# Cross-attention and ternary FFN on one core: the first context block loaded in rows and turned by TensorE, its projection in contraction halves

## What is computed

```python
q = ctx @ Wq.T + bq                    # 512 x 128, key likewise with Wk, bk
attention = softmax(q @ key.T)         # 512 x 512
x = x + layernorm(x) @ attention.T
w1q, w2q = ternary(w1), ternary(w2)    # clip(round(w / mean|w|), -1, 1)
h = gelu(layernorm(x) @ w1q.T + b1)    # 512 x 2048
x = x + h @ w2q.T + b2
```

## Time and profile before

| | us |
|---|---|
| median of 3 runs | 312.29 |
| lowest, highest | 311.95, 313.38 |
| profiled execution | 312.49 |
| its span (first to last instruction) | 310.70 |
| TensorE busy | 303.9 |
| VectorE, ScalarE, GpSimd busy | 153.7, 143.9, 109.2 |

### The profile page before, as it was taken

The page is one execution under the profiler, slowest core; times in us unless marked ns, Lnnn a source line. Parts: engine busy times, 40 slices in busy tenths (PEclk is TensorE's granted clock), DMA queues, the critical chain, the costliest instruction groups (busy, mean ns, idle before and its releaser), DMA issues.

```text
span 310.7 us, 3674 instructions
## 1 busy us (share of the span) xinstructions
PE 303.9 (98%) x1401; PEld 144.2 (46%) x1401; DVE 153.7 (49%) x295; ACT 143.9 (46%) x253; POOL 109.2 (35%) x111
## 2 busy tenths in 40 slices
PE   6799999999999999999999999999999999999996
PEld 3366544444444444444444444444444444444455
DVE  0888896764598853755308342445433003442101
ACT  2179998577723506542654604545440017762000
POOL 0276339999979960000903620000650000000000
PEclk9999999999999999999999999999999999999999
DMA  7899999674653992000032854000034100000011
GB/s 174 237 381 408 361 277 205 131 135 103 121 104 63 155 228 105 2 0 0 0 70 54 166 103 154 0 0 0 2 69 115 56 34 0 0 2 0 34 49 54
DMA packets 66706, 32.24 MB, mean 104 GB/s; under 512 B 59504, under 2 KB 60032, under 8 KB 66176
## 3 DMA queue, kind: packets, MB, share of 16 engines
q1 hardware_dynamic: 66368, 31.73, 40.4%
q10 hardware_dynamic: 320, 0.27, 0.4%
HBM read 15.21 MB, written 4.19 MB: 62 GB/s over the span
## 4 chain that ended last, share of the span: by engine, by line
PE 96%; DMA 2%; DVE 1%; SPq 0%; ACT 0%; issue 0%
PE ps_t L511 36%; PE ps_e L536 24%; PE ps_e L494 13%; PE ps_e L525 9%; PE ps_e L443 5%; PE ps_e L435 2%; PE ps_e L543 2%; PE ps_t L435 2%; DMA ctx_sb<-in_ctx 2%; PE ps_t L467 1%; PE ps_e L454 1%; PE ps_t L454 1%; SPq L247 0%; DVE ctxT L764 0%; ACT qkT L644 0%; DVE x_sb L1055 0%
## 5 line engine op out<-in xcount | busy, mean ns | idle before, releaser
L511 PE MATMUL ps_t<-x2T,w1T 128*128 128x512 f16 x512 | 112.1, 379 | 0.0
L706 ACT ACTIVATE ps_t<-ps_t,b_col 128x512 f32<-128x512 f32 x64 | 42.5, 665 | 96.6 <-PE ps_t L511 96.6
L511 PEld LDWEIGHTS ps_t<-x2T,w1T 128*128 128x128 f16 x512 | 50.1, 98 | 60.7 <-issue 0.6
L900 DVE SCALAR_TENSOR_TENSOR gT_lo<-ps_t,h_scale,gT_hi 128x512 f16<-128x512 f32 x64 | 45.1, 746 | 66.2 <-ACT gT_hi L711 66.2
L536 PE MATMUL ps_e<-w_raw,gT_hi 128*128 128x512 f16 x176 | 66.7, 379 | 0.0
L536 PE MATMUL ps_e<-w_raw,gT_lo 128*128 128x512 f16 x176 | 66.7, 379 | 0.0
L349 POOL TENSOR_TENSOR rstd<-var_eps,minus_half 128x4 f32<-128x4 f32 (+1 forms) x9 | 8.5, 947 | 99.7 <-DVE neg_mean L813 99.7
L711 ACT ACTIVATE gT_hi<-ps_t,h_scale 128x512 f16<-128x512 f32 x64 | 40.3, 684 | 0.0
L906 DVE SCALAR_TENSOR_TENSOR x_sb<-ps_e,h_unscale,x_sb 128x512 f32<-128x512 f32 x15 | 11.0, 748 | 57.9 <-PE ps_e L536 54.6
L536 PEld LDWEIGHTS ps_e<-w_raw,gT_lo 128*128 128x128 f16 x176 | 17.2, 98 | 21.4 <-issue 1.0
L536 PEld LDWEIGHTS ps_e<-w_raw,gT_hi 128*128 128x128 f16 x176 | 17.2, 98 | 21.1 <-issue 0.7
(11 more groups left out here) (86 smaller groups left out, 290.9 us busy)
## 6 DMA issues: line engine op xcount, KB each, us to landing
w_raw<-in_L_ffn_w SPq DMA_DIRECT2D x8, 1024.0 KB, 14.7
x_sb<-in_x SPq DMA_DIRECT2D x4, 1024.0 KB, 7.5
out<-x_sb SPq DMA_DIRECT2D x15, 256.0 KB, 2.6
ctx_sb<-in_ctx SPq DMA_DIRECT2D x16, 128.0 KB, 3.2
b_sb<-in_L_ffn_b SPq DMA_DIRECT2D x1, 256.0 KB, 7.2
w_raw<-w_raw SPq DMA_TRANSPOSE x16, 3.8
out<-x_sb SPq DMA_DIRECT2D x2, 128.0 KB, 1.7
x2n<-in_L_xattn_Wq ACTq DMA_DIRECT2D x1, 128.0 KB, 3.0
```

Source lines behind the costliest of these rows:

```text
L511: mm = nc.tensor.matmul(ps_t[t][:], w1T[:, k, j], x2T[:, b % 2, v, :, j], start=(v == 0 and j == 0), stop=(v == 1 and j == ND - 1))
L706: nc.scalar.activation(ps_t[t][:], ps_t[t][:], ACT.Gelu, scale=1.0 / LN_SCALE, bias=b1_col[:, k:k + 1]).then_inc(gelu_done, 1)
L900: nc.vector.scalar_tensor_tensor(out=gT_lo[:, k], in0=ps_t[t][:], scalar=h_scale[:, 0:1], in1=gT_hi[:, k], op0=ALU.mult, op1=ALU.subtract) ...
```

## The change

- ctx of batch 0 is loaded in rows: two DMAs of 128 partitions, each with two rows of 256 floats per partition. It is turned by eight TensorE transposes into PSUM banks `ps_t0` and `ps_t1`, one bank for each contraction half k, and VectorE copies each bank into `ctxT` with one instruction. Batches 1 to 3 keep the old way.
- The projection of batch 0 runs by contraction halves: half 0 of k and q after the first copy, half 1 of k and q after the second. k comes ahead of q, in banks `ps_t3` and `ps_t2`.
- ScalarE copies k first, then the first 128 columns of q, then the other 384. The first tile of the scores waits for the first two of these copies only.
- The four matmuls on zeros behind the transposes are gone. The transpose of b1 moves behind the projection, the sum over b1 behind the scores.
- SyncE issues the two tiny loads of bq and bk ahead of x of batch 0.

```diff
@@ load queue (SyncE)
+            def load_ctx0():
+                rows = ctx_in[0].rearrange("(t p) c -> p t c", p=P)
+                for h in range(2):
+                    sp.dma_start(ctx0_rows[:, 2 * h:2 * h + 2], rows[:, 2 * h:2 * h + 2]).then_inc(ctx0_here[h], 16)
...
-            load_ctx(0)
-            load_x(0)
+            load_ctx0()
             sp.dma_start(bqk[:, 0:1], bq.rearrange("(p a) -> p a", a=1)).then_inc(bqk_here, 16)
             sp.dma_start(bqk[:, 1:2], bk.rearrange("(p a) -> p a", a=1)).then_inc(bqk_here, 16)
+            load_x(0)
             load_ctx(1)
@@ TensorE
+            def first_projection():
+
+                for h in range(2):
+                    pe.wait_ge(ctx0_here[h], 16)
+                    for k in range(NC):
+                        for t in (2 * h, 2 * h + 1):
+                            mm = nc.tensor.transpose(ps_t[k][:, t * P:(t + 1) * P], ctx0_columns[:, t, k], ident[:])
+                        if h == 1:
+                            mm.then_inc(ctx0T_ready, 1)
+                pe.wait_ge(WT_done, 1)
+                pe.wait_ge(ctx0T_done, 1)
+                for s in (1, 0):
+                    nc.tensor.matmul(qk_bank(0, s)[:], WT[:, s, 0], ctxT[:, 0], start=True, stop=False)
+                pe.wait_ge(ctxT_ready, 1)
+                for s in (1, 0):
+                    nc.tensor.matmul(qk_bank(0, s)[:], WT[:, s, 1], ctxT[:, 1], start=False,
+                                     stop=True).then_inc(qk_ready, 1)
...
             mm.then_inc(WT_ready, 1)
+            first_projection()
             pe.wait_ge(b1_here, 16)
             nc.tensor.transpose(ps_e[3][:, 0:NF], b1_rows[:], ident[0:NF, 0:NF]).then_inc(b1T_ready, 1)
-            warm_up(WARM_UP_2)
-            pe.wait_ge(WT_done, 1)
-            project(0, lambda s: None)
-
-            total(B1, ps_t[3])
 
             def free(t):
-                if t == 3:
+                if t == 1:
+                    pe.wait_ge(qkT_done, 3)
+                elif t == 3:
                     pe.wait_ge(b1_col_done, 1)
             scores(0, range(NT), free)
+            total(B1, ps_t[3])
             project(1, lambda k: None)
@@ ScalarE
+            def copy_first_qk():
+
+                for s, columns, n in ((1, slice(0, L), 1), (0, slice(0, P), 2), (0, slice(P, L), 2)):
+                    act.wait_ge(qk_ready, n)
+                    nc.scalar.activation(qkT[:, s, columns], qk_bank(0, s)[:, columns], ACT.Identity,
+                                         bias=bqk[:, s:s + 1]).then_inc(qkT_done, 1)
...
-            copy_qk(0)
+            copy_first_qk()
@@ VectorE
+            def copy_turned_ctx0():
+                for k, done in enumerate((ctx0T_done, ctxT_ready)):
+                    dve.wait_ge(ctx0T_ready, k + 1)
+                    nc.vector.tensor_copy(ctxT[:, k], ps_t[k][:]).then_inc(done, 1)
...
-            turn_ctx(0)
+            copy_turned_ctx0()
             b1_columns()
             moments(0)
             turn_ctx(1)
```

More of the change, by code:

```diff
@@ L21 @@
 WARM_UP = 10
-WARM_UP_2 = 4
 ROUND = 1.5 * 2.0 ** 23
@@ L66, in xattn_ffn @@
         ctx_sb = sb("ctx_sb", [P, L // R, C // Q])
+        ctx0_rows = ctx_sb[:].rearrange("p a b -> p (a b)").rearrange("p (t c) -> p t c", t=NT)
+        ctx0_columns = ctx0_rows.rearrange("p t (i k) -> p t k i", k=NC)
         ctxT = sb("ctxT", [P, NC, L])
@@ L150, in xattn_ffn @@
         W_here, b1_here, bqk_here, ctx_here = sem("W_here"), sem("b1_here"), sem("bqk_here"), sem("ctx_here")
+        ctx0_here = [sem(f"ctx0_here{h}") for h in range(2)]
         x_here = [sem(f"x_here{b}") for b in range(B)]
@@ L168, in xattn_ffn @@
         WT_ready, b1T_ready, total_ready = sem("WT_ready"), sem("b1T_ready"), sem("total_ready")
+        ctx0T_ready = sem("ctx0T_ready")
         qk_ready, scores_ready = sem("qk_ready"), sem("scores_ready")
@@ L182, in xattn_ffn @@
         xn0_read = sem("xn0_read")
+        ctx0T_done = sem("ctx0T_done")
         ctxT_ready, b1_col_done, b1_abs_done = sem("ctxT_ready"), sem("b1_col_done"), sem("b1_abs_done")
@@ L204, in qk_bank @@
         def qk_bank(b, s):
-            return ps_t[s] if b in (1, EARLY) else ps_e[s]
+            if b == 0:
+                return ps_t[2 + s]
+            return ps_t[s] if b <= EARLY else ps_e[s]
         def scores_bank(b, t):
@@ L242, in _ @@
         def _(sp):
+            def load_ctx0():
+                rows = ctx_in[0].rearrange("(t p) c -> p t c", p=P)
+                for h in range(2):
+                    sp.dma_start(ctx0_rows[:, 2 * h:2 * h + 2], rows[:, 2 * h:2 * h + 2]).then_inc(ctx0_here[h], 16)
             def load_ctx(b):
-                if b:
-                    sp.wait_ge(ctxT_ready, b)
+                sp.wait_ge(ctxT_ready, b)
                 for q in range(Q):
@@ L425, in _ @@
         def _(pe):
-            def warm_up(times):
-                for _ in range(times):
-                    nc.tensor.matmul(ps_e[0][:], gT_lo[:, 0, 0:P], gT_lo[:, 0], start=True, stop=True)
+            def first_projection():
[14 more added lines that the diff above has]
+                                     stop=True).then_inc(qk_ready, 1)
             def project(b, free):
@@ L439, in scores @@
             def scores(b, tiles, free):
-                pe.wait_ge(qkT_done, 2 * b + 2)
+                pe.wait_ge(qkT_done, 2 * b + 3 if b else 2)
                 for t in tiles:
@@ L462, in turn_probs @@
                     elif j < 2:
-                        pe.wait_ge(qkT_done, 2 + j + 1)
+                        pe.wait_ge(qkT_done, 3 + j + 1)
                     elif j == 3:
@@ L548, in _ @@
             pe.wait_ge(zeros_done, 1)
-            warm_up(WARM_UP)
+            for _ in range(WARM_UP):
+                nc.tensor.matmul(ps_e[0][:], gT_lo[:, 0, 0:P], gT_lo[:, 0], start=True, stop=True)
             pe.wait_ge(ident_done, 1)
@@ L759, in _ @@
         def _(dve):
+            def copy_turned_ctx0():
+                for k, done in enumerate((ctx0T_done, ctxT_ready)):
+                    dve.wait_ge(ctx0T_ready, k + 1)
+                    nc.vector.tensor_copy(ctxT[:, k], ps_t[k][:]).then_inc(done, 1)
             def turn_ctx(b):
-                dve.wait_ge(ctx_here, 16 * Q * (b + 1))
-                if b:
-                    dve.wait_ge(qk_ready, 2 * b)
+                dve.wait_ge(ctx_here, 16 * Q * b)
+                dve.wait_ge(qk_ready, 2 * b)
                 nc.vector.transpose(ctxT[:].rearrange("p k (tb r) -> p tb k r", r=R),
```

## The result

The changed kernel takes 313.76 us (median of 20 runs, 313.11 to 314.34), the kernel before 312.54 us (20 runs beside them, 311.43 to 314.39). The ratio is 1.0038, interval 1.0024 to 1.0052: 0.8 to 1.6 us slower. The forecast was 313.2, within 312.0 to 314.9.

What follows compares the result with a forecast made beforehand. TensorE, busy 303.9 of 310.70 us, bounds the kernel, with a VectorE-ScalarE chain only about 0.15 us ahead of it. The terms 1.3 - 0.28 - 0.15 = +0.87 us give 312.29 + 0.9 = 313.2 us, range 312.0 to 314.9.

Steps and rivals of the forecast that it cites:

- Landing and turn of ctx: Start of batch 0: ctx lands at 6.3, first projection matmul starts at 7.5 instead of 9.28.
- The early branch of the forecast: With ctx landing early, its turn after 5.85 and the copy set the first projection matmul at 7.3; total +0.7 us.
- Projection, copies, scores: TensorE and ScalarE, batch 0: scores start near 11.5 instead of 13.73, 2.2 us won on TensorE there.
- b1's turn, the deciding term: VectorE's queue waits for b1's transpose behind the projection; moments of x start at 11.8 instead of 10.49, 1.3 us late.
- about where it was: Issue of x of batch 0: two fewer ctx issues but two tiny ones ahead; x no longer releases the moments.
- Where the 2.2 us go: Scores of batch 0 to total(W1): TensorE's waits use up its lead, exponentials recover 0.28; total(W1) starts at 42.5.
- The slack of 0.15: At total(W1): VectorE-ScalarE chain about 0.15 us ahead of TensorE (41.49 against 41.64), subtracted from the lateness.
- (a): Rival: TensorE's early scores pass through to the end, 312.29 - 2.2 = 310.1 us; chance 0.04.
- (b): Rival: VectorE's 0.70 us idle at 19.00 and earlier landings soak up most lag, +0.2, 312.5 us; chance 0.19.
- (c): Rival: ctx lands as late as today (7.86), matmuls start at 9.1, VectorE 2.9 late, 314.8 us; chance 0.14.
- (d): Rival: TensorE's clock falls or never rises for the projection, which takes 3.43 us more, 316.6 us; chance 0.06.

Runs made afterwards that it cites:

- e3: Kernel before with k projected ahead of q, q copied in two pieces and scores after the first piece: 312.01 us, ratio 0.9992.
- e2: Kernel before with two extra VectorE passes over x of batch 0 ahead of the moments: 313.31 us, ratio 1.0047.
- e1: Changed kernel with b1's transpose ahead of the projection: 313.23 us, ratio 1.0042 to the kernel before.
- e5: e1 with the sum over b1 ahead of the scores as well: 312.54 us, ratio 1.0000 to the kernel before.
- e10: Changed kernel, VectorE order only: moments before b1's columns, first maximum before ctx 1's turn, gelu scale after maxima: 312.50 us, ratio 1.0019 to the kernel before.
- e12: e10 with the loads of bq and bk behind x again: 311.02 us, ratio 0.9966 to the kernel before.
- e9: Changed kernel with only the sum over b1 ahead of the scores, b1's transpose left late: 313.87 us, ratio 1.0059 to the kernel before.
- e11: Changed kernel run again without edits, beside e9 and e10: 313.83 us, ratio 1.0059 to the kernel before.
- e8: e4 with 3 instead of 10 matmuls on zeros at the start: 311.80 us, ratio 0.9989 to the kernel before.
- e4: e1 plus x of batch 0 in halves, first maximum before ctx 1's turn, gelu scale after maxima: 311.31 us, ratio 0.9967 to the kernel before.
- e6: e4 with x of batch 0 in one load: 311.44 us, ratio 0.9974 to the kernel before.
- e7: Kernel before with e4's x halves and VectorE order alone: 312.32 us, ratio 0.9990.

## Why the prediction was right, and where its size was off

- **Landing and turn of ctx**: first projection matmul at 7.30, forecast 7.5, early bound 7.3. The landing was better than the 6.3 of the forecast: ctx took about 4.0 us from its issues and was there by about 5.4, so that its transposes followed those of W at 5.54 without a wait. The early branch of the forecast, in which the W transposes set the start, is the one that came true.
- **Projection, copies, scores**: 11.42, forecast 11.5. e3 shows that the copy in pieces gives its 0.3 us to TensorE and nothing measurable to the end (its interval, 0.9974 to 1.001, could hide 0.3 us; the fixed 48.5 behind the moments speaks against it). ScalarE's three copies together took 1.63 us from 10.21.
- **b1's turn, the deciding term**: VectorE was released at 11.16 (forecast 11.25) and started the moments at 11.67 (11.8). e2 reproduces the loss by lateness of VectorE alone, and e1 with e5 undoes it by moving b1's two steps back. That x no longer released the moments was right here, but narrowly: it landed 8.3 us after its issue at 2.72, at 11.02, not near 10.45. The issue was indeed where it had been (2.75 before), but "about where it was" is wrong for the landing: by e10 and e12, the two bias loads ahead of x delay it. So of the 1.18 by which VectorE is late b1's turn added 0.65, and 0.53 would have been there without it. In e9 x was even the later of the two.
- **Where the 2.2 us go**: wait for ctx 1 0.65 (forecast 0.85), first maximum 16.36 (16.5), probabilities 0.38 (0.4), batch 1's maxima 27.74 (27.9), total(W1) 42.35 (42.5), FFN 60.17 (60.2). The exponentials of batch 0 won back 0.28 as worked out (17.07 to 19.07).
- **The slack of 0.15** was not there. It came from comparing two kinds of starts: 41.64 in the earlier trace rows is where the matmul ahead ends, while the record of `total(W1)` itself begins earlier, because matmuls are pipelined (timeline of TensorE, kernel before):

```profile
41.50 0.35 PE L473 MATMUL ps_t<-abs_row,ones 128*128 128x1 f32 x2
```

  That is the same 0.35 us and the same 0.29 behind the start of `abs_row` as in the changed kernel (42.06 to 42.35). VectorE's chain and TensorE arrived together, and the 0.85 by which `abs_row` moved is the 0.85 by which the FFN moved. The expectation of e1 reads the same 0.21 and 0.35 as a restart of a waiting TensorE; that reading is wrong too, since the record is 0.35 long in both kernels.
- **Why the sum came out**: the forecast was 1.3 - 0.28 - 0.15 = 0.87. Measured it is 1.18 for the moments, less 0.33 caught up before batch 1's maxima (26.89 to 27.74), less nothing at `total(W1)`: 0.85. A lateness that was too large and a slack that was not there cancel, so that the 0.02 between forecast and profile is luck; the mechanism is the one forecast.
- **Size**: the forecast was +0.9 and the profiles moved by 0.85, the medians by 1.2 and in the second measurement by 2.0. Two things lie outside the pair of profiles. The kernel before varies with x and ctx: e3, which has the same loads, had FFN 1.4 us earlier than its profile. And the changed kernel has executions like e11, where TensorE's clock rose later (below) and all started 0.8 later. Its 20 timed runs fall in two groups of ten, 313.11 to 313.67 and 313.86 to 314.34, with the first profile (313.33) in one and e11's (314.15) at the place of the other; that the clock makes these groups is likely, but the other runs have no trace.
- **Rivals**: (a) and (b) fell. (c), a late ctx, did not occur in any profile of the new load: the first projection matmul behind it came at 7.24 to 8.10 with ten zero matmuls, and at 8.10 (e11) the clock was the cause, not the landing: the W transposes ended later there, and ctx had been there since about 5.7. (d) did not occur in the changed kernel's first profile (four half matmuls in 1.95 us). The profile of e8 shows it as real once the zeros are too few. By the rule of the Trainium skill ("TensorE: Matmul & The Clock Gate", Part 4) that transposes do not count as activity the way matmuls do, it should be so. e8 does not contradict it, but is weak evidence: thirteen transposes in 5.12 to 8.13 did not raise the clock, and in e11 ten real matmuls in 4.45 us had not raised it either.

## What to carry over

A step taken out of TensorE's way is not free if another engine's queue stands behind it: b1's 16 columns cost TensorE 0.2 us and held VectorE for 0.65 us beyond the landing of x, because VectorE's in-order queue kept its old place for them. When the bounding engine starts earlier, compute the slack of each chain that joins it later (here none at `total(W1)`), and compare records of one kind when doing so; reorder the waiting engine's queue by what arrives first, and keep tiny scattered loads behind the large one that the chain waits for. e4 and e6 reorder the queue, e12 does both, and all three are about 1 us faster than the kernel before, and so faster than the changed one.

## What the hardware showed that I had not expected

- Two loads of 0.5 KB, one float to each partition, ahead of a 1 MB load: x landed 8.3 us after its issue with them ahead (e10), 6.6 with them behind (e12). Over all profiles with x in one load it took 6.9 to 9.4 us with them ahead (seven profiles) and 6.6 to 7.7 with them behind (four, three of them with the old load of ctx), so single executions overlap. Why they cost that much the traces do not settle.
- The moment at which TensorE's clock rises differs between executions of the same kernel. In the changed kernel's first profile the ten zero matmuls took 3.93 us and four W transposes 0.72; in e11, the same program, it was (timeline of TensorE)

```profile
1.17 4.45 PE L574 MATMUL ps_e<-gT_lo 128*128 128x512 f16 x10 [1.17 <-DVE gT_lo L945]
5.41 1.06 PE L580 MATMUL ps_e<-ident,x2n 128*128 128x128 f32 x4
6.27 1.20 PE L442 MATMUL ps_t<-ident,ctx_sb 128*128 128x128 f32 x8
8.10 1.96 PE L448 MATMUL ps_t<-ctxT,WT 128*128 128x512 f32 x4 [0.64 <-DVE ctxT L794]
```

  with all ten at 0.43 us (1.2 GHz) and the W transposes at the lower clock too. The projection began 0.8 us later and the FFN 0.82 later. The change itself opened the kernel to this: in e7, with the old load of ctx, the zero matmuls and W transposes took the same 4.45 and 1.06 us, and the projection still started 0.14 us behind the end of VectorE's turn of ctx. fp32 transposes do depend on the clock: eight took 1.91 us in e8 and 1.12 in e4. The granted clock of the profile reads 1.00 in all of this.
